# Layer 0 attention: the second head pair's probabilities are scaled on VectorE instead of GpSimd

## The reference

```python
x = x + L0_xattn(layernorm(x), ctx_512, Wq, Wkv_expand, Wout)
# inside: 16 heads of 32, 256 queries and 256 keys per batch element, causal
scores = einsum('bhqd,bhkd->bhqk', qh, kh) / sqrt(32), masked above the diagonal
attn = softmax(scores)
out = einsum('bhqk,bhkd->bhqd', attn, vh); out @ Wout.T
```

## Time and profile before

| | us |
|---|---|
| median of 3 runs | 1177.27 (1176.14 to 1177.8) |
| the profiled execution, its own time | 1180.87 |
| its span, first to last instruction | 1178.9 |
| mean granted TensorE clock | 0.945 |
| busy over the whole span: TensorE | 1001.1 |
| VectorE | 790.7 |
| ScalarE | 654.2 |
| GpSimd | 184.3 |

### The profile page before, as it was taken

How to read it: one execution, slowest core, us unless ns; L and a number is a source line. 1 busy time by engine, 2 the same in 40 slices (tenths; PEclk the granted TensorE clock), 3 DMA queues, 4 the chain that set the end, 5 groups by cost and what they waited for, 6 DMA issues and landing times. The chain is left out here.

```text
span 1178.9 us, 20926 instructions
## 1 busy us (share of the span) xinstructions
PE 1001.1 (85%) x7516; PEld 783.9 (66%) x7516; DVE 790.7 (67%) x1729; ACT 654.2 (55%) x1687; POOL 184.3 (16%) x183
## 2 busy tenths in 40 slices
PE   0789999998129989786999999999999999995763
PEld 0778888876114444344888888888878888884652
DVE  5467776664768889625666777677767767674663
ACT  2477777765457776545545555555545545542542
POOL 0555555443000000012001010101001010000000
PEclk9999999998659999998999999999999999997887
DMA  6400000000437000051000000000000000000011
GB/s 236 157 6 7 6 6 7 1 2 1 143 105 234 0 0 0 1 197 37 19 1 19 2 19 1 21 1 4 16 3 18 1 1 1 1 1 1 18 54 71
DMA packets 19679, 41.79 MB, mean 35 GB/s; under 512 B 896, under 2 KB 4224, under 8 KB 19072
## 3 DMA queue, kind: packets, MB, share of 16 engines
q1 hardware_dynamic: 16944, 32.14, 8.4%
q10 hardware_dynamic: 2640, 8.39, 1.9%
HBM read 36.33 MB, written 4.19 MB: 34 GB/s over the span
## 5 line engine op out<-in xcount | busy, mean ns | idle before, releaser
L1322 ACT ACTIVATE probs<-c_score,c_neg_max 128x256 f32<-128x256 f32 x256 | 119.1, 481 | 15.9 <-DVE c_neg_max L1383 14.0
L1308 ACT ACTIVATE c_h<-c_bank_b 128x512 fp32r<-128x512 f32 x64 | 38.2, 597 | 153.7 <-PE c_bank_b L1240 153.7
L526 POOL TENSOR_TENSOR a_probs<-a_probs,a_inv 128x256 f32<-128x256 f32 (+1 forms) x128 | 102.7, 828 | 107.4 <-DVE a_inv L584 107.4
L434 ACT ACTIVATE a_probs<-a_s,a_neg_max 128x128 f32<-128x128 f32 (+1 forms) x256 | 104.0, 433 | 26.6 <-DVE a_neg_max L572 26.0
L1096 POOL TENSOR_TENSOR c_ctx_raw<-c_ctx_raw,c_table 128x1024 f32<-128x1024 f32 x8 | 19.1, 2383 | 597.9 <-PE c_bank_b L1240 357.6
L1373 DVE TENSOR_TENSOR c_l<-c_bank_b,c_h 128x512 fp32r<-128x512 f32 x64 | 44.2, 691 | 99.2 <-ACT c_h L1308 99.2
L44 PE MATMUL c_acc<-VO_h,c_l 128*128 128x512 f32 x256 | 100.8, 394 | 1.9 <-DVE c_l L1373 1.9
L1313 ACT ACTIVATE c_pT_h<-c_turn 128x512 fp32r<-128x512 f32 x128 | 69.7, 596 | 55.6 <-PE c_turn L1230 55.6
L46 PE MATMUL c_acc<-VO_h,c_h 128*128 128x512 f32 x256 | 100.5, 393 | 0.0
L45 PE MATMUL c_acc<-VO_l,c_h 128*128 128x512 f32 x256 | 100.0, 391 | 0.0
L1378 DVE TENSOR_TENSOR c_pT_l<-c_turn,c_pT_h 128x512 fp32r<-128x512 f32 x128 | 81.8, 679 | 2.6 <-ACT c_pT_h L1313 2.6
(11 more groups left out here) (250 smaller groups left out, 2784.9 us busy)
## 6 DMA issues: line engine op xcount, KB each, us to landing
g_x<-in_x ACTq DMA_DIRECT2D x4, 1024.0 KB, 15.8
w_raw<-in_w ACTq DMA_DIRECT2D x1, 4096.0 KB, 14.1
w_raw<-in_w SPq DMA_DIRECT2D x4, 1024.0 KB, 9.1
wq<-in_wq SPq DMA_DIRECT2D x1, 4096.0 KB, 23.0
c_ctx_raw<-in_ctx SPq DMA_DIRECT2D x8, 512.0 KB, 3.4
wo<-in_wo SPq DMA_DIRECT2D x1, 4096.0 KB, 14.2
out<-g_x SPq DMA_DIRECT2D x8, 512.0 KB, 2.8
aw_raw<-in_wq SPq DMA_DIRECT2D x1, 1024.0 KB, 7.7
```

The source lines that it names most:

```text
L434: last = act.activation(probs[i % 2][:, 2 * pair + j, at], s[:, 2 * pair + j, at], ACT.Exp, bias=neg_max[:, pair, q, j:j + 1], accum_out=s ...
L526: last = pool.tensor_tensor(p, p, inv[:, pair, q, :].unsqueeze(2).broadcast_to([P, 2, (q + 1) * P]), ALU.mult)
L1322: last = act.activation(probs[p % 2][:, i, :], score[h][:, t, :], ACT.Exp, bias=neg_max[:, i:i + 1], accum_out=sums[:, i:i + 1])
```

## The change

The second pair's multiplication leaves GpSimd and goes to VectorE, directly behind the second reciprocal, with a drain between them, since the product reads what the reciprocal wrote. The transposes TZ and TX wait for a semaphore of their own. The reciprocal of the second pair no longer waits for GpSimd and no longer signals it.

```diff
-                    pe.wait_ge(normed, 2 * slot + (1 if kind == "TY" else 2))
+                    if kind == "TY":
+                        pe.wait_ge(normed, slot + 1)
+                    else:
+                        pe.wait_ge(normed_dve, slot + 1)
...
-                    for pair in range(2):
-                        pool.wait_ge(inverted, 2 * (b * 4 + i) + pair + 1)
-                        for q in range(2):
-                            p = probs[i % 2][:, 2 * pair:2 * pair + 2, q * P:(2 * q + 1) * P]
-                            last = pool.tensor_tensor(p, p, inv[:, pair, q, :].unsqueeze(2).broadcast_to([P, 2, (q + 1) * P]),
-                                                      ALU.mult)
-                        last.then_inc(normed, 1)
+                    pool.wait_ge(inverted, b * 4 + i + 1)
+                    for q in range(2):
+                        p = probs[i % 2][:, 0:2, q * P:(2 * q + 1) * P]
+                        last = pool.tensor_tensor(p, p, inv[:, 0, q, :].unsqueeze(2).broadcast_to([P, 2, (q + 1) * P]), ALU.mult)
+                    last.then_inc(normed, 1)
...
-                    if slot > 0:
-                        dve.wait_ge(normed, 2 * slot + pair - 1)
-                    dve.reciprocal(inv[:, pair, :, :], sums[:, pair, :, :]).then_inc(inverted, 1)
+                    if pair == 0:
+                        if slot > 0:
+                            dve.wait_ge(normed, slot)
+                        dve.reciprocal(inv[:, 0, :, :], sums[:, 0, :, :]).then_inc(inverted, 1)
+                        return
+                    dve.reciprocal(inv[:, 1, :, :], sums[:, 1, :, :])
+                    dve.drain()
+                    for q in range(2):
+                        p = probs[i % 2][:, 2:4, q * P:(2 * q + 1) * P]
+                        last = dve.tensor_tensor(p, p, inv[:, 1, q, :].unsqueeze(2).broadcast_to([P, 2, (q + 1) * P]), ALU.mult)
+                    last.then_inc(normed_dve, 1)
```

More of the change, by code:

```diff
@@ L261, in layer0_attention @@
         weighted, c_hi, c_lo = m.sem("weighted"), m.sem("c_hi"), m.sem("c_lo")
-        put_out, added = m.sem("put_out"), m.sem("added")
+        put_out, added, normed_dve = m.sem("put_out"), m.sem("added"), m.sem("normed_dve")
         steps = [step for step in steps_of_layer0()]
```

## The result

The changed kernel takes 1192.3 us (median of 4 runs, 1190.67 to 1195.44) against 1176.9 for the kernel before in the same comparison. The ratio is 1.0125 with a 95% interval from 1.0106 to 1.0145, a loss of 15.4 us (12.5 to 17.1). The forecast was 1189.1 us, a loss of 11.9, in a range of 1183.5 to 1196.5. Direction and mechanism held; one wait stood at another place than forecast, and the clock took a part that the sum did not have in it.

A forecast was written before the change was run, and what follows sets the result against it. TensorE was taken to set the pace, with VectorE's strict queue deciding what is delayed. Terms of 5.6 + 2.9 + 2.15 + 1.2 = 11.85 us on the 1177.27 us median gave 1189.1 us, range 1183.5 to 1196.5.

The forecast's parts named there:

- Rival (a): VectorE's 48 idle us of 160 swallow the moved work: 1177.3 us, within 0.2%; chance 0.09.
- Rival (b): Faster, since products are ready sooner and the context subtraction falls from 0.83 to 0.42 us: 1174.2 us; chance 0.03.
- Element 0, slot 0: VectorE's products wait for GpSimd's first pair, so the subtraction TensorE already waits for comes 1.15 us later.
- its slot 2: Slot 2 of element 0: TensorE already waits 1.20 us for c_l, so the whole pair shows, 1.0 us.
- Slot 2 of elements 1 to 6: c_l stands behind the pair and TensorE's transposes need its bank: 0.5 us each, 2.9 in all.
- Slot 3 to slot 0: Maxima and yT_l come later behind the second reciprocal: 0.8 us at each of seven transitions, 5.6 in all.
- The last element: Element 7: maxima at slot 2 come 0.7 us later, a copy behind slot 3's pair 0.5 more; together 1.2 us.
- The pair with its drain: Drain and two products hold VectorE 1.02 us per slot, with bounds of 0.85 and 1.15.
- Slots 0 and 1: In steady elements, existing room or idle time on VectorE covers the added products: 0 us.
- The step that was wrong in its place: Slot 3 to slot 0: TensorE's 0.24 us wait for yT_l at transposes L346 grows by 0.8 us.
- the second half of rival (c): The clock falls behind a longer TensorE gap, 1 to 3 us for one fall; chance 0.15 for all of (c).
- The first half of rival (c): GpSimd's y holds VectorE's products in slot 1 of elements 0 to 4: 5.9 us more, 1195; (c) chance 0.15.

The follow-up runs named there:

- slots 0 and 1: VectorE scales the second pair in slots 0 and 1 only, GpSimd in slots 2 and 3; ratio 1.0014 to the kernel before.
- 21 pairs: VectorE scales the second pair in slots 0 to 2 of elements 1 to 7, slot 2's products later in its queue; ratio 1.0033 to the kernel before.
- the variant of slots 2 and 3: VectorE scales the second pair in slots 2 and 3 only, GpSimd in the others; ratio 1.0106 to the kernel before.
- y first: The kernel before, GpSimd scaling both pairs, with y's low half in slot 0 ahead of the second pair of maxima; ratio 0.9989 to the kernel before.
- the variant from element 1: VectorE scales the second pair from element 1 on, element 0 is left to GpSimd; ratio 1.0092 to the kernel before.
- the one-input variant: As the changed kernel, but GpSimd scales the first pair with four one-input instructions in place of two two-input ones; one run, 1191.94 us.

## Why the prediction was right, and where not

**The bound and the mechanism.** TensorE set the pace and VectorE's order decided; both were shown, by slots 0 and 1 at no cost in the steady elements and by 21 pairs placed in idle time with TensorE's 158.51 us unchanged. Rival (a), that VectorE's 48 idle us swallow the work, is right about those places and wrong about the other two. Rival (b), a gain from products that are ready sooner, found no place: the context subtraction did fall to 0.41 us, and the time rose.

**The terms, by the trace.** Element 0, slot 0: 1.15 forecast, 1.19 measured; its slot 2: 1.0, measured 0.93 in the variant of slots 2 and 3, where the clock held until there. Slot 2 of elements 1 to 6: 0.5 each, measured 0.51 to 0.60. Slot 3 to slot 0: 0.8 each, measured 0.64 to 0.78. The last element: 1.2, measured 0.76 at the 3.57 us wait and 0.54 at the copy behind it, 1.3. The pair with its drain: 1.02, measured 1.02 from the end of the reciprocal (111.20) to the next instruction (112.22). Slots 0 and 1: 0, measured 0.01 over five elements. Together the forecast terms measured 11.8 us against 11.85.

**The step that was wrong in its place.** "TensorE's last transposes of slot 3 (L346) already wait 0.24 us for yT_l ...: the wait grows by 0.8." It did not grow; it fell to at most 0.2. TensorE stopped earlier, at L321 for qk_l, a wait of 0.82 that had no row before because the two met there. The price came out near since both stand behind the same products on VectorE; that 0.8 and 0.75 agree so well is in part luck. In elements 6 and 7, which turn no y, TensorE waits for qk_l as well, at the product with the values (1.7 us in two waits).

**What the sum had left out.** Slot 2 of element 0 cost 1.75 in place of 1.0, and from there to slot 0 of element 1 another 1.55 went that no term had. Windows of the kernel after:

```profile
60.00:63.00 3.00, 1.20 (x24) 1.14 (x24) 1.42 (x5) 2.93 (x12) 2.67 (x3) 0.85 0.00 0
63.00:66.00 3.00, 3.00 (x27) 1.94 (x27) 2.34 (x5) 0.74 (x5) 1.76 (x1) 0.58 0.17 49
66.00:69.00 3.00, 3.00 (x35) 2.75 (x27) 1.30 (x5) 2.73 (x14) 1.61 (x2) 1.00 0.00 0
69.00:72.00 3.00, 1.52 (x30) 1.17 (x28) 2.77 (x6) 1.70 (x4) 0.00 (x0) 1.00 0.00 0
72.00:75.00 3.00, 3.00 (x23) 2.20 (x17) 1.99 (x6) 1.08 (x4) 1.01 (x1) 0.56 0.00 0
```

TensorE was busy 1.20 of 3 us and then 1.52 of 3, and behind each the clock was at its lower level, 1.2 GHz, for most of a window. That is the second half of rival (c), some 2.3 us, within the 1 to 3 allowed for one fall but in two. Whether the change brings them is not shown. The first fall is in seven of the ten profiles, also in those of 21 pairs and of y first, which leave element 0 as it was; there it cost at most 0.2 us. A window of y first:

```profile
63.00:66.00 3.00, 3.00 (x24) 1.90 (x24) 2.34 (x6) 2.33 (x13) 1.97 (x2) 0.54 0.15 44
```

The second is in two of the four profiles that have slot 2's products directly behind the reciprocal in element 0, and in no other. The other way, a fall in the last element cost the kernel before 2.6 us, measured against the variant from element 1, which had none there, and the kernel after 1.3. The 0.9 us that the prediction read for it came from its first 3 us alone; the next two windows of the kernel before:

```profile
267.00:270.00 3.00, 1.95 (x15) 1.33 (x8) 1.80 (x5) 2.28 (x12) 0.00 (x0) 0.50 0.03 5
270.00:273.00 3.00, 3.00 (x10) 2.31 (x10) 0.00 (x0) 1.32 (x7) 1.61 (x2) 0.67 0.00 0
```

So 12.3 = 11.85 + 2.3 - 1.3 - 0.6, the last being an earlier start of the stage, as unplanned as the clock. That the sum met the attention's 12.3 us within half a microsecond is luck in that part: three terms that it did not have nearly cancel.

**The first half of rival (c).** "If y holds VectorE's products" happened in part. Slot 1 of element 1 in the kernel after, VectorE and GpSimd:

```profile
94.66 1.42 DVE L592 TENSOR_TENSOR a_probs<-a_probs,a_inv 128x256 f32<-128x256 f32 x2
...
96.60 0.41 DVE L550 TENSOR_TENSOR a_cT_l<-a_ctx_raw,a_cT_h 128x256 fp32r<-128x256 f32 x1
```

```profile
94.44 2.08 POOL L520 TENSOR_SCALAR y<-g_x,g_mean_var,g_rstd 128x512 f32<-128x512 f32 x1
```

A product that began 0.22 us after y took 0.4 longer, not the whole 2 us of y, and it cost nothing, since slot 1 has room. The pair takes 1.42 to 1.45 us in slot 1 of elements 1 to 4, which have a y there, and 1.03 in elements 5 to 7, which have none. The Trainium skill (GPSIMD Engine Reference, Key points) has contention for VectorE instructions with two SBUF inputs and makes no exception for GpSimd's one-input instructions; these rows agree with it, but the row at 33.92 in the earlier trace rows and the one-input variant show none, and the price depends on the moment.

**The rest of the measured loss.** The medians say 15.4 (12.5 to 17.1), the attention of the profile 12.3. The 2.5 us behind L127 are inside what equal code varied by, 6 us over ten profiles. The 0.6 left lies between the two profiled executions, 14.8 apart, and the medians. That the change has a part in them was neither shown nor excluded.

## What to carry to other kernels

Work that is moved to an engine with idle time is paid by where in its queue it stands: list what is queued behind it and the idle time between, place by place, since here, in the steady elements, half of the pairs were free and the other half cost 0.5 to 0.8 us each. When a queue is late, every instruction in it is late, so the wait appears at the consumer that comes first, also where the profile before shows no wait because two events met exactly. A fall of the clock moved single profiles here by up to 2.6 us whatever the edit was, so compare first the stretches that ran at the same clock, and the end of a stage only after.

## What the hardware showed that was not expected

GpSimd's two-input product keeps VectorE's two-SBUF-input product standing until it ends (0.83 us in place of 0.42). It goes the other way too: at 61.93 us of the kernel after, y began together with VectorE's pair of 1.04 us, which was not slowed; GpSimd's timeline:

```profile
61.93 2.83 POOL L520 TENSOR_SCALAR y<-g_x,g_mean_var,g_rstd 128x512 f32<-128x512 f32 x1
```

y took 2.83 us in place of 2.08. On VectorE four one-head instructions with a per-partition scalar took as long as two tensor products, 1.01 against 1.03 us.
